# Retention's group norm and output projection moved into its loop, and first operations of two stages issued inside the norms ahead of them

## The reference

```python
x = x + 0.5 * mixture_of_experts(layernorm(x))
x = x + softmax_attention(layernorm(x))           # 16 heads of 8 channels
x = x + 0.5 * mixture_of_experts(layernorm(x))
x = x + 0.5 * two_local_layers(layernorm(x))      # each: local attention, norm, gated FFN
x = x + retention(layernorm(x))                   # 16 heads of 8 channels
x = x + 0.5 * two_local_layers(layernorm(x))
```

```python
qk  = einsum(q, k) / sqrt(8) * decay              # lower triangle only
out = einsum(qk, v)
out = (out - out.mean(head)) * rsqrt(out.var(head) + 1e-5)   # group norm, per head of 8
out = out * gn_weight + gn_bias
return out @ Wo.T
```

## Time and profile before

| | |
|---|---|
| median of 3 runs | 2470.07 us (2469.4 to 2472.6) |
| the profiled execution, its own time | 2490.64 us |
| its span, first to last instruction | 2488.8 us |
| PE busy in the span | 2306.8 us (93%) |
| DVE / ACT / POOL busy | 1863.5 / 1804.7 / 1479.0 us |
| retention, first to last multiplication by the triangle | 1565.71 to 1684.82 us |
| from there to the end of the local layers' norm | 1684.82 to 1732.12 us |

### The profile page before, as it was taken

One profiled execution on the slowest core, in us unless ns is written; L12 is line 12 of the kernel. 1 busy time (PEld: TensorE's weight loads), 2 busy tenths in 40 slices (PEclk: granted clock), 3 DMA queues, 4 the chain that ended last, 5 costly groups with the idle time before them and its releaser, 6 DMA issues. The chain is left out here.

```text
span 2488.8 us, 65430 instructions
## 1 busy us (share of the span) xinstructions
PE 2306.8 (93%) x21510; PEld 1696.3 (68%) x21510; DVE 1863.5 (75%) x4164; ACT 1804.7 (73%) x5994; POOL 1479.0 (59%) x1402
## 2 busy tenths in 40 slices
PE   5796999997796999999999999887999999999999
PEld 3793666664794888854888854673788864788863
DVE  3694888884684999964999964784899973899974
ACT  3354888883355999973999974335999982999982
POOL 4572777773572777841787850330877750778760
PEclk7897999997898999999999999999999999999999
DMA  6111000000112000000000000000000000000000
GB/s 229 46 48 40 2 0 0 0 1 26 50 47 97 8 6 8 6 3 3 10 7 8 6 0 0 1 1 5 10 7 6 8 1 4 8 8 6 8 1 34
DMA packets 34262, 47.47 MB, mean 19 GB/s; under 512 B 6384, under 2 KB 27760, under 8 KB 33744
## 3 DMA queue, kind: packets, MB, share of 16 engines
q1 hardware_dynamic: 29584, 36.45, 4.7%
q0 software_dynamic: 4544, 9.35, 1.2%
HBM read 24.44 MB, written 12.96 MB: 15 GB/s over the span
## 5 line engine op out<-in xcount | busy, mean ns | idle before, releaser
L248 POOL TENSOR_TENSOR space<-space,tabs 128x512 f32<-128x512 f32 x256 | 326.3, 1275 | 309.8 <-DVE space L347 293.7
L273 ACT ACTIVATE space<-psum,space 128x128 f32<-128x128 f32 x1024 | 358.6, 360 | 8.4 <-DVE space L351 8.4
L245 POOL TENSOR_TENSOR space<-space 128x512 f32<-128x512 f32 x256 | 266.6, 1041 | 160.3 <-DVE space L335 160.3
L252 POOL TENSOR_TENSOR space<-space 128x512 f32<-128x512 f32 x256 | 325.2, 1270 | 26.8 <-POOL space L248 7.6
L159 PE MATMUL psum<-space,big 128*128 128x256 f32 x1024 | 266.5, 383 | 12.5 <-DVE space L347 12.2
L926 POOL TENSOR_TENSOR space<-space 128x256 f32<-128x256 f32 (+1 forms) x256 | 221.4, 886 | 82.9 <-DVE space L1027 80.8
L331 DVE CAST psum<-cb 128x512 f32<-128x512 bf16 x256 | 177.9, 695 | 88.9 <-ACT space L273 88.9
L182 PE MATMUL psum<-space,cf 128*128 128x384 f32 x512 | 210.2, 492 | 1.9 <-DVE space L317 1.5
L971 ACT ACTIVATE space<-psum,space 128x128 f32<-128x128 f32 (+1 forms) x512 | 210.2, 442 | 1.7 <-DVE space L1020 1.7
L273 ACT ACTIVATION_READ_ACCUMULATOR space<-psum,space 128x1 f32 x1024 | 204.8, 200 | 0.0
L159 PEld LDWEIGHTS psum<-space,big 128*128 128x128 f32 x1024 | 176.0, 192 | 30.6 <-issue 17.1
(11 more groups left out here) (193 smaller groups left out, 5652.2 us busy)
## 6 DMA issues: line engine op xcount, KB each, us to landing
big<-early SPq DMA_DIRECT2D x1, 6688.0 KB
space<-sorted_x SPq DMA_DIRECT2D x78, 64.5 KB
z<-token_y SPq DMA_DIRECT2D x16, 256.0 KB, 5.2
space<-z SPq DMA_DIRECT2D x64, 64.0 KB, 1.9
space<-z SPq DMA_DIRECT2D x64, 63.8 KB, 2.0
big<-late SPq DMA_DIRECT2D x1, 3114.0 KB, 15.4
x<-x_t SPq DMA_DIRECT2D x4, 512.0 KB, 5.8
x_final<-x SPq DMA_DIRECT2D x8, 256.0 KB, 2.0
```

The lines of the kernel that those rows point to most:

```text
L245: pool.tensor_tensor(x, x, rl[:, (j - 3) % 2, :, :].rearrange("p h t -> p (h t)").unsqueeze(2).to_broadcast([P, 4, P]), ALU.mult).then_inc ...
L248: pool.tensor_tensor(tS[:, :], t2[:, :], tab[:, 1, :], ALU.mult).then_inc(ts_ready, 1)
L252: pool.tensor_tensor(t3[:, j % 2, :], t1[:, j % 2, :], tS[:, :], ALU.add).then_inc(summed, 1)
L273: ins = act.activation(pr[:, (j - 3) % 2, h, t * P:(t + 1) * P], s_ps[h][:, t * P:(t + 1) * P], ACT.Exp, bias=nm[:, (j - 3) % 2, h, t:t + ...
```

## The change

- `retention` gets the output weights, gain and bias. In its loop, for each batch: the result of batch b-1 is centred per head into the second half of its own `ol` bank (TensorE, 256 columns), squared (ScalarE), its variance goes into the first half of that bank (TensorE), then logarithm and exponential (ScalarE), the product with the centred values into `nb` (VectorE `normalise`), gain and bias (ScalarE, into `sc`), the output projection into bank 0 (TensorE) and the addition to x (VectorE `residual`). These stand one, two and three batches behind. TensorE's `project(b+2)` moves from r=0 to r=1. ScalarE's four masked keys are split two and two around gain and bias.
- The group norm's `layer_norm` and the second `project_residual` are gone; the local layers' norm after retention has no feed.
- The norms ahead of `small_head_softmax` and of `retention` use three centring banks instead of four (1, 2, 3 and 2, 3, 6), which leaves bank 0 to the stage behind. That stage's first operations are issued by each engine inside the norm (`early`): on TensorE the first projection after step 4, the first values after step 6 (and retention's second projection after step 8), on VectorE the first rotation after normalisation 4, on ScalarE the first bias and values.
- With a feed, VectorE runs feed steps 0 to 3, and then before each normalisation u feed step u+4 (`FED`).

```diff
-    NB, VB = 4, 2
+    NB, VB = len(banks[0]), len(banks[1])
+    FED = 4
...
+    def meanwhile(engine, eng, s):
+        for start in early.get((engine, s), ()):
+            start(eng)
...
     def vector(dve):
         if feed is not None:
-            feed.vector(dve, 0)
-            feed.vector(dve, 1)
+            for u in range(FED):
+                feed.vector(dve, u)
         for u in range(U):
-            if feed is not None and u + 2 < U:
-                feed.vector(dve, u + 2)
+            if feed is not None and u + FED < U:
+                feed.vector(dve, u + FED)
             dve.wait_ge(r_ready, S0 + u + 1)
...
+        stages.append(layer_norm(nc, g, of("norm"), room, g.x, g.hn, g.center, g.mean, prev=stages[-1], turn=4, banks=((2, 3, 6), (4, 5)), early=early))
...
-        stages.append(layer_norm(nc, g, of("norm"), room, g.hn, g.hn, g.head_center, g.head_mean, gain=g.r1_gain, bias=g.r1_bias,
-                                 prev=stages[-1], load_table=False, turn=5, gained=2))
-        stages += half(stages[-1], 1, project_residual(nc, g, of("project"), g.r1_wo, None, (6, 7), stages[-1], 1))
+        stages += half(stages[-1], 1, None)
```

In retention's loops (TensorE, ScalarE, VectorE):

```diff
+                if r == 1 and runs(b + 2, B):
+                    if at_least(b, 3):
+                        pe.wait_ge(x_ready, b - 2)
+                    tensor_project(pe, b + 2)
...
-                if r == 0 and runs(b + 2, B):
-                    project(b + 2)
+                if r == 0 and runs(b - 3, B):
+                    pe.wait_ge(scaled, b - 2)
+                    pe.wait_ge(turned, min(b + 2, B) if isinstance(b, int) else b + 2)
+                    if at_least(b, 4):
+                        pe.wait_ge(x_ready, b - 3)
+                    mm(head_ps[:, 0:T], wo, sc[:, 1 - k, :], start=True, stop=True).then_inc(moved, 1)
+                if runs(b - 1, B):
+                    if r == 0:
+                        pe.wait_ge(out_ready, b)
+                        mm(ol[1 - k][:, T:2 * T], g.head_center, tokens(g.hn, b - 1), start=True, stop=True).then_inc(c_ready, 1)
+                    else:
+                        pe.wait_ge(sq_ready, b)
+                        mm(ol[1 - k][:, 0:T], g.head_mean, sq, start=True, stop=True).then_inc(var_ready, 1)
...
+                        act.activation(lnv, ol[k][:, 0:T], ACT.Ln, bias=g.tiny[:, 2:3]).then_inc(ln_ready, 1)
...
+                        act.activation(rstd, lnv, ACT.Exp, scale=-0.5).then_inc(r_ready, 1)
...
+                        act.activation(sc[:, k, :], nb, ACT.Identity, bias=bias, scale=gain).then_inc(scaled, 1)
...
+                        act.activation(sq, ol[1 - k][:, T:2 * T], ACT.Square).then_inc(sq_ready, 1)
...
                     for jl in range(2):
+                        if r == 0 and jl == 1 and runs(b - 2, B):
+                            normalise(b - 2, k)
                         dve.tensor_tensor(pr[:, r, jl, :, :], g.bank_quad3[:, :, jl * T:(jl + 1) * T], g.tri_01.unsqueeze(1).to_broadcast([P, 4, T]), ALU.mult).then_inc(p_ready, 1)
...
                 if r == 0 and runs(b, B):
                     state(b, k)
+                if r == 0 and runs(b - 3, B):
+                    residual(b - 3)
```

More of the change, by code:

```diff
@@ L432, in constants, with layer_norm @@
     return f, b
-def layer_norm(nc, g, sem, room, src, dst, center, mean, shift=False, gain=None, bias=None, load=None, prev=None, load_table=True, turn=0, shifted=0, gained=0, feed=None):
+def layer_norm(nc, g, sem, room, src, dst, center, mean, shift=False, gain=None, bias=None, load=None, prev=None, load_table=True, turn=0, shifted=0, gained=0, feed=None, banks=((0, 1, 2, 3), (4, 5)), early=None):
     W = 2 * T
     U = N // W
-    NB, VB = 4, 2
+    NB, VB = len(banks[0]), len(banks[1])
+    early = {} if early is None else early
     LAG = 2
+    FED = 4
     S0, SH0, G0 = turn * U, shifted * U, gained * U
@@ L444, in layer_norm @@
     var_ready, ln_ready, r_ready, normed_ready, done = sem("var_ready"), sem("ln_ready"), sem("r_ready"), sem("normed_ready"), sem("done")
-    cb, vb = g.bank[0:NB], g.bank[NB:NB + VB]
+    cb, vb = ([g.bank[k] for k in ks] for ks in banks)
+    def meanwhile(engine, eng, s):
+        for start in early.get((engine, s), ()):
+            start(eng)
     def part(x, s):
@@ L485, in tensor @@
                 if s < NB and prev is not None:
-                    prev.free(pe, s)
+                    prev.free(pe, banks[0][s])
                 if s >= NB:
@@ L536, in free @@
     def free(eng, bank):
[L537 to L540, removed]
+        if bank in banks[0]:
+            last = max(u for u in range(U) if banks[0][u % NB] == bank)
+            eng.wait_ge(normed_ready, S0 + last + 1)
+        elif bank in banks[1]:
+            last = max(u for u in range(U) if banks[1][u % VB] == bank)
+            eng.wait_ge(ln_ready, S0 + last + 1)
         elif feed is not None:
@@ L712, in layers @@
         stages, collected = sparse(1, begin, None)
-        stages.append(layer_norm(nc, g, of("norm"), norm_room, g.x, g.hn, g.center, g.mean, prev=collected, feed=collected, turn=0))
+        early = {}
+        stages.append(layer_norm(nc, g, of("norm"), norm_room, g.x, g.hn, g.center, g.mean, prev=collected, feed=collected, turn=0,
+                                 banks=((1, 2, 3), (4, 5)), early=early))
         stages.append(small_head_softmax(nc, g, of("ss"), ss_room, g.l0_w.rearrange("p (n c) -> p n c", n=3), l0_tab, g.l0_qkv_b, stages[-1],
-                                         lambda pool: collected.there(pool, 0)))
+                                         lambda pool: collected.there(pool, 0), early))
         moved, collected2 = sparse(2, None, project_residual(nc, g, of("project"), g.l0_wp, g.l0_bp, (5, 6), stages[-1], 0))
@@ L778, with small_head_softmax @@
 TRI = 384
-def small_head_softmax(nc, g, sem, room, w, tab, bias, prev, room_free):
+def small_head_softmax(nc, g, sem, room, w, tab, bias, prev, room_free, early):
     U = B * EACH
@@ L814, in of, with tensor_project, tensor_values @@
         return b if e >= lag else b - 1
-    def tensor(pe):
[L817 to L834, removed]
+    def tensor_project(pe, b):
+        if at_least(b, 1):
+            pe.wait_ge(v_ready, b)
+        if is_first(b):
+            prev.there(pe, 0)
+            prev.free(pe, 0)
+        if isinstance(b, int) and b == 1:
+            prev.there(pe, B // 2 - 1)
+        for n in range(2):
+            ins = mm(head_ps[:, n * T:(n + 1) * T], w[:, n, :], tokens(g.hn, b), start=(n == 0), stop=(n == 1), skip_group_check=True)
+        ins.then_inc(proj_ready, 1)
+    def tensor_values(pe, b):
+        pe.wait_ge(h_ready, b + 1)
+        pe.wait_ge(xb_ready, b + 1)
+        for t in range(2):
+            ins = mm(head_ps[:, t * P:(t + 1) * P], hT[:, t * P:(t + 1) * P], w[:, 2, :], start=(t == 0), stop=(t == 1), skip_group_check=True)
+        ins.then_inc(vp_ready, 1)
+    def tensor(pe):
         def body(i):
@@ L895, in body @@
                     ins.then_inc(pv_ready, 1)
-        project(0)
-        values(0)
         rounds(pe, 1, B // 2 - 1, 2, body)
@@ L1060, in small_head_softmax, with retention @@
     return Stage(sync=nothing, tensor=tensor, scalar=scalar, vector=vector, gpsimd=gpsimd, there=there, free=free)
-def retention(nc, g, sem, room, w, tab, prev, room_free):
+def retention(nc, g, sem, room, w, tab, wo, gain, bias, prev, room_free, early):
     ROUNDS = 2
```

252 lines of the change are left out of this document (144 added, 108 removed).

## The result

| | before | changed |
|---|---|---|
| median | 2469.35 us (2468.09 to 2472.6, 6 runs) | 2454.88 us (2451.28 to 2460.84, 6 runs) |
| ratio | | 0.9943, 95% interval 0.9926 to 0.996 |
| profiled execution, own time | 2490.64 us | 2457.18 us |

The account below looks back on a forecast made before the run. Retention's loop was taken as a relay of TensorE scores and VectorE multiplications, fed norms as a ring through three engines. Terms -7.7, -2.1, +2.3, +15.5, -21.9 sum to -13.9: median 2470.07 to 2456.2 us, range 2446 to 2467.

Parts of the forecast that it names:

- Term 1: Norm after the second experts, four banks, feed four ahead: addition leaves the ring, step 2.16 us; -7.7 us.
- Term 2: Norm after the first experts, three banks, feed four ahead: no gain per step, but queries begin earlier; -2.1 us.
- The ring: Chain of waits through three engines from centring to centring: 3.82 us after the first experts, 3.05 before retention.
- Term 3: Norm before retention, three banks, no feed: step 3.05 us instead of 1.72, partly regained at retention's start; +2.3 us.
- Term 4: Retention's loop: r=0 4.10 us set by VectorE, r=1 4.40 by TensorE, period 8.5; +15.5 us.
- Term 5: Behind the loop: group norm and projection gone, a tail and plain norm remain, 25.4 instead of 47.3; -21.9 us.
- The tail: New chain behind retention's last multiplication, from last product through copy, norm and projection to the addition: 6.5 us.
- The half clock: TensorE nearly idle in the tail behind retention, clock at 0.50 as at retention's start: 2.3 us added.
- Rival A: Retention's loop: TensorE overlaps more, only VectorE's 0.35 us is added; period 7.9, 2447.8 us; chance 0.14.
- C: Retention's loop: three new products run one behind the other; period 10.1, +8.5 us, 2478.6 us; chance 0.08.
- D: Fed norm after the second experts: transposes wait for gathered rows, feed gains nothing; 2463.9 us; chance 0.04.
- B: Three-bank norms: clock at 1.2 GHz adds 4.3 us before retention, 8.6 after first experts; 2469 us; chance 0.12.

Follow-up runs that it names:

- experiments 5 to 8: Changed kernel unedited (ratio 0.9958); with `normalise` behind both multiplications (0.9938); with the variance product issued twice (8.87 us a batch); with the centring product issued twice (8.68).
- experiment 2: Changed kernel with the feed two steps ahead again instead of four: ratio 0.9979 to the kernel before, -6.6 us.
- experiments 6 to 8: Changed kernel with one loop edit each: `normalise` behind both multiplications (8.25 us a batch), variance product issued twice (8.87), centring product issued twice (8.68).
- experiment 5: Changed kernel again, unedited, on a second chip: ratio 0.9958 to the kernel before, -11.2 us.
- experiments 8 and 10: Changed kernel with the centring product issued twice (8.68 us a batch); changed kernel with four centring banks in both norms and `normalise` behind both multiplications (ratio 0.9882).
- experiment 3: Changed kernel with four centring banks instead of three in both norms: ratio 0.9885 to the kernel before, -27.5 us.

## Why the prediction was right

- **Term 1** (-7.7): measured -8.3. The step is 2.16 as worked out; the rest lies in the first steps and doesn't repeat (21.65 to 21.74 us for the stage in experiments 5 to 8, -7.8).
- **Term 2** (-2.1): -2.5. The ring was 3.86, not 3.82. The longer lead gained nothing. The gain is that of the early operations: experiment 2 has the kernel before's step of 3.65 and three banks, and its queries still start 2.8 us earlier.
- **Term 3** (+2.3): +2.5. The ring was 3.12, not 3.05, since a centring starts 0.15 us after the normalisation that it waits for (1518.26 after 1518.11), not 0.05. In the five other profiles with three banks the stage is 24.74 us, +2.0: the first scores took 1.17 us there and 1.75 in the changed kernel's first profile, where the clock fell to its lower level under them.
- **Term 4** (+15.5): +15.1. Both halves had the limits named, 4.08 against 4.10 and 4.36 against 4.40; experiments 6 to 8 test each of them. The twelve batches at the period took 8.44 us instead of 8.5 each, and the first 10.59 instead of 10.2.
- **Term 5** (-21.9): -21.7, by two errors that cancel. The tail was 7.3 us, not 6.5: from start to next start the seven operations of ScalarE and VectorE took 0.50 us each where I had put some 0.4 (gain and bias 0.65, the last addition 0.57), and centring, variance and projection 0.73 where I had put 0.63. The half clock came, but late and short, and cost some 1.7 us instead of 2.3.
- **Rival A** (period 7.9) and **C** (10.1) are out by the period of 8.44, **D** by the step of 2.16. **B** is out: through the three-bank norm before retention two-pass products stay at 1.02 to 1.10 us, the length of 2.4 GHz, and the granted clock is 1.00 with TensorE at work for 14.58 of 19.17 us:

```profile
1512.33:1531.50 19.17, 14.58 (x37) 6.18 (x36) 5.81 (x10) 10.35 (x18) 0.40 (x1) 1.00 0.00 0
```

In the other three-bank norm it is 1.00 too from the third centring to the last. By the Trainium skill's section on psum-queue depth-cycling (TensorE: Matmul & The Clock Gate) the clock could have gone back and forth there; the trace does not agree.

That the median came within 1.3 us of the forecast is partly luck. The changed kernel's six times lie in two groups, 5 to 9 us apart (last section), with the median between them, and on the second chip the difference was 11.2 us and not 14. What is shown is the sum of the stages, -14.9 against -13.9, and the limits in them. The forecast of 2476.7 us for the profiled execution failed: it took the 20.6 us by which the profile before lies above its median for something that the next profile would have too.

What the prediction did not ask was whether the parts needed each other. Its own ring sum held the larger finding: the addition could leave the ring in the kernel before too.

## What to carry to other kernels

When a pipelined loop is slower than any engine in it, add up the ring from a buffer's fill to its release; how far ahead a feed runs and how many buffers there are set the step, and one line may do what a restructuring does. Moving a stage's work into another loop pays only what the host loop's limiting engine has idle: here 1.3 us of TensorE into 0.7 us of room (+0.61 in r=1) and 0.33 us of VectorE into none (r=0) made each batch 0.95 us longer and gave back two thirds of what was won behind it. Taking a buffer away to make room for early work should be priced by the ring, not by the engine's load.

## What the runs showed of the hardware

The changed kernel's six times fall apart into 2451.3 to 2452.6 and 2457.2 to 2460.8 us. A possible cause of such steps can be seen in its profile: at the end of the second local attention of the first half the granted clock goes to the 1.2 GHz level with TensorE at work, after a wait of 1.78 us:

```profile
1424.00:1426.00 2.00, 2.00 (x33) 1.65 (x25) 1.12 (x2) 0.83 (x5) 0.73 (x1) 0.65 0.00 0
1426.00:1428.00 2.00, 1.48 (x7) 0.92 (x7) 0.51 (x2) 1.06 (x5) 0.15 (x1) 0.50 0.00 0
```

It stayed there for some 10 us, as it did in experiments 8 and 10; in four other profiles it fell there for 3.5 us, and in five not at all. That stretch, from the norm's end behind the second experts to the last addition to x before retention, was 756.77 us long in this profile, and 752.34 in that of experiment 5 on the same code; the other ten profiles lie between these. The kernel before has the same wait, 1.79 us, at the same place, and stays at full clock.

The way back differs too. These are 18 us of softmax attention's start, from some 15 us behind the first queries on, in the changed kernel and in experiment 3:

```profile
233.50:251.50 18.00, 18.00 (x162) 12.20 (x160) 13.46 (x32) 13.94 (x63) 11.63 (x14) 0.91 0.01 3
```

```profile
236.00:254.00 18.00, 18.00 (x106) 11.27 (x103) 10.33 (x21) 9.46 (x42) 7.67 (x9) 0.54 0.00 1
```

TensorE counts as busy for all 18 us in both, at 0.91 and at 0.54 of the clock. In windows of 0.5 us, the clock stood at its lower level for 17 us behind the first queries in five profiles, for some 24 in three and for 30.5 in two, and softmax attention was 308.2, 311 and 314.3 us long in them, so up to 6 us of what a change wins ahead of it can be given back. What decides when the clock falls and returns in such a case was not tested.
